# First attention's opening reordered; feed-forward weights quantised inside its loop; layer-norm statistics one sequence per step

## The reference

```python
def _mha(q, k, v, mask):                      # 16 heads of 16 columns
    scores = einsum('bhqd,bhkd->bhqk', qh, kh) / sqrt(16)
    scores = scores + mask[:, None] * -10000.0
    return einsum('bhqk,bhkd->bhqd', softmax(scores), vh)

def lpbq_dequant(w):                          # blocks of 32, 4 bits
    s = maximum(max(abs(wb), axis=-1) / 7, 1e-12)
    return clip(round(wb / s), -8, 7) * s

x = x + _mha(layernorm(x), ctx, ctx, mask)
x = x + ffn(layernorm(x), w_gate, w_up, w_down)   # weights through lpbq_dequant
x = x + xattn(layernorm(x), ctx, ctx, Wq, ...)
x = x + moe(layernorm(x), W1, b1, W2, b2, Wr, br) # 8 experts, top 1
```

## Time and profile before

| what | value |
|---|---|
| median of 3 runs (range) | 1606.71 us (1605.7 to 1612.56) |
| span of the profiled execution | 1606.6 us |
| first attention, first transfer to the start of the feed-forward | 0.8 to 302.8 us |
| start of the first row maximum (step 0) | 40.85 us |
| start of the row maximum of step 4 (first of the loop) | 80.91 us |
| start of the row maximum of step 28 (first behind the loop) | 264.62 us |
| busy over the span: PE, DVE, ACT, POOL | 1336.5, 1215.0, 1030.7, 416.9 us |

### The profile page before, as it was taken

One profiled execution on the slowest core, in us unless ns is written; L12 is line 12 of the kernel. 1 busy time (PEld: TensorE's weight loads), 2 busy tenths in 40 slices (PEclk: granted clock), 3 DMA queues, 4 the chain that ended last, 5 costly groups with the idle time before them and its releaser, 6 DMA issues. The chain is left out here.

```text
span 1606.6 us, 36137 instructions
## 1 busy us (share of the span) xinstructions
PE 1336.5 (83%) x11579; PEld 1171.7 (73%) x11579; DVE 1215.0 (76%) x2159; ACT 1030.7 (64%) x2751; POOL 416.9 (26%) x655
## 2 busy tenths in 40 slices
PE   3688888599973039699999999999999728999996
PEld 2355555488852039688999998999899628999996
DVE  5777777667879997567777777777777777888885
ACT  2578887555578446366676666666667506888885
POOL 2433333100000000402322222222222243555553
PEclk9899999799997569899999999999999859999998
DMA  6411111000042103600111111111100047411110
GB/s 197 152 35 33 39 31 35 15 1 0 0 139 71 39 22 118 208 8 21 34 37 51 34 33 33 33 33 40 39 29 28 21 171 272 153 46 54 50 45 10
DMA packets 61009, 96.76 MB, mean 60 GB/s; under 512 B 9083, under 2 KB 47998, under 8 KB 58113
## 3 DMA queue, kind: packets, MB, share of 16 engines
q1 hardware_dynamic: 55938, 83.15, 15.5%
q0 software_dynamic: 4992, 12.60, 2.5%
HBM read 76.57 MB, written 21.90 MB: 61 GB/s over the span
## 5 line engine op out<-in xcount | busy, mean ns | idle before, releaser
L1695 ACT ACTIVATE c_w_raw<-c_ps_score,c_shift 128x128 f32<-128x128 f32 x512 | 184.6, 397 | 133.0 <-DVE c_shift L1550 130.6
L2081 PE MATMUL d_ps_hT<-d_zT,d_w_tile 128*128 128x128 f32 x1248 | 147.9, 277 | 2.3 <-DVE d_zT L2186 2.3
L2081 PEld LDWEIGHTS d_ps_hT<-d_zT,d_w_tile 128*128 128x128 f32 x1248 | 144.8, 194 | 2.9 <-DVE d_zT L2186 2.9
L840 PE MATMUL b_ps<-b_down_high,b_inner 128*128 128x256 f32 x384 | 71.0, 288 | 89.1 <-DVE b_inner L1122 89.1
L2254 ACT ACTIVATE d_h<-d_ps_hT,d_b1T 128x128 f32<-128x128 f32 x312 | 88.8, 366 | 65.1 <-PE d_ps_hT L2081 65.1
L840 PEld LDWEIGHTS b_ps<-b_down_high,b_inner 128*128 128x128 f32 x384 | 60.6, 194 | 89.5 <-issue 89.5
L2094 PE MATMUL d_ps_y<-d_w_parts,d_hT 128*128 128x256 f32 x936 | 122.9, 288 | 1.8 <-DVE d_res L2217 1.8
L484 DVE TENSOR_REDUCE a_row_max<-a_ps_score 128x8 f32<-128x1024 f32 x64 | 77.9, 1218 | 58.5 <-PE a_ps_score L395 58.5
L1695 ACT ACTIVATION_READ_ACCUMULATOR c_w_raw<-c_ps_score,c_shift 128x1 f32 x512 | 120.9, 236 | 0.0
L2094 PEld LDWEIGHTS d_ps_y<-d_w_parts,d_hT 128*128 128x128 f32 x936 | 115.8, 193 | 2.0 <-DVE d_res L2217 2.0
L1418 PE MATMUL c_ps_proj<-c_ctxT,c_wk 128*128 128x256 f32 x768 | 107.7, 290 | 4.9 <-ACT c_qT L1717 3.3
(11 more groups left out here) (260 smaller groups left out, 3665.7 us busy)
## 6 DMA issues: line engine op xcount, KB each, us to landing
d_w<-w_in SPq DMA_DIRECT2D x16, 1024.0 KB, 7.0
b_x_space<-w_in SPq DMA_DIRECT2D x16, 512.0 KB, 3.5
zx_scratch<-c_zx SPq DMA_DIRECT2D x32, 256.0 KB, 2.4
a_x<-x_in SPq DMA_DIRECT2D x4, 1024.0 KB, 7.5
a_keys<-ctx_blocks_in SPq DMA_DIRECT2D x128, 32.0 KB, 2.1
a_v_raw<-ctx_in SPq DMA_DIRECT2D x4, 1024.0 KB, 8.7
x_scratch<-a_x SPq DMA_DIRECT2D x32, 128.0 KB, 1.7
b_x_space<-x_scratch SPq DMA_DIRECT2D x32, 128.0 KB, 2.4
```

What stands on the lines that cost most here:

```text
L840: last = pe.matmul(ps[:, t, 0:D], inner[:, s, a, f, t * P:(t + 1) * P], down_parts[b][:, f, :], start=(j == 0), stop=(j == NF * len(PARTS) ...
L1695: last = act.activation(prob[:, n, j, :], ps_score[:, n % 2, j, :], ACT.Exp, scale=float(KD) ** -0.5, bias=shift[:, n, j:j + 1], accum_out ...
L2081: last = pe.matmul(ps_hT[:, f, :], w1_tile[:, half, k, n * P:(n + 1) * P], zT[:, s, k, :], start=(k == 0), stop=(k == ND - 1))
```

## The change

- The block for the identity matrix goes; SP loads it second, and PE waits for it ahead of its first transpose.
- SP's opening order becomes: x of sequences 0 and 1, identity, mask, half the keys of the first pair (ACT's queue starts the other half), x of 2 to 7, values, keys of the second pair, the other parts of x and of the mask, and the three weight matrices last. The clearing of the key buffer on POOL is split into two halves.
- The opening quantisation goes. The weights have a buffer of their own, and DVE quantises half a matrix (128 by 768) in each of the 6 passes of the loop: maxima and scale in its first step, reciprocal and product in its second, rounding in its third, product in its fourth. PE's 36 transposes and ACT's copies (now 9 of 512 columns where 36 of 128 were) move into the steps behind the last sequence.
- Statistics for the first eight sequences are taken at the start (two, then six); for the others DVE takes those of sequence b+4 in step b of its loop, and POOL adds two small operations to each step from 4 to 27.

DVE in the opening, before: `w_scale`, `w_inv` are the scales of the weights, `yT` holds the raw weights, `prob` and `probT` serve as scratch.

The diff, cut:

```diff
+        X_PARTS = ((0, 2), (2, 8), (8, 16), (16, 24), (24, 32))
-                load_weights(sp, 0)
-                load_weights(sp, 1)
                 load_x(0)
-                load_weights(sp, 2)
+                sp.dma_start(ident[:], eye).then_inc(ident_loaded, 16)
                 load_mask(0)
-                sp.wait_ge(keys_zero, 1)
-                load_keys(0, 0)
-                load_keys(1, 1)
+                load_first_keys(sp, 0, 0, range(0, HALF, 2))
+                load_x(1)
                 load_v(0)
-                for c in range(1, 4):
+                load_first_keys(sp, 1, 1, range(HALF))
+                for c in range(2, 5):
                     load_x(c)
-                    if c < 3:
-                        load_mask(c)
+                    if c < 4:
+                        load_mask(c - 1)
+                for n, (w, _) in enumerate(weights):
+                    sp.dma_start(w_sb[:, n]..., w...).then_inc(w_loaded, 16)
...
+                def deviation_ahead(b, u):                       # POOL
+                    pool.wait_ge(mv0_done, b + 5)
+                    pool.tensor_tensor(var_next[:, u:u + 1], mv_next[:, u, 1:2], eps[:], ALU.add)
+                    pool.wait_ge(var0_done, b - 1)
+                    pool.tensor_tensor(rstd_next[:, u:u + 1], var_next[:, u:u + 1], power[:, 0:1], ALU.pow)
...
                     if inside(b, 2, NB + 1):
                         residual(b - 2, s)
                         inverse_deviation(b - 2, s)
+                    if inside(b, 4, NB - 5):
+                        deviation_ahead(b, u)
                     if inside(b, 1, NB - 2):
                         values(b + 1, 1 - s)
...
+                def statistics_ahead(b, u):                      # DVE
+                    dve.wait_ge(q_centred, b + 1)
+                    dve.bn_stats(stats_next[:], x_sb[:, b + 4, :]).then_inc(ahead_done, 1)
+                    dve.wait_ge(ahead_done, b - 3)
+                    dve.bn_aggr(mv_next[:, u, :], stats_next[:]).then_inc(mv0_done, 1)
+
+                def quantise(i, u):
+                    half = w_halves[:, bass.ds(i - 1, 1)]
+                    if u == 0:
+                        dve.wait_ge(w_loaded, 16 * MATS)
+                        dve.tensor_reduce(w_scale[:], half, AX_X, ALU.max, ...)
+                        dve.tensor_scalar(w_scale[:], w_scale[:], 1.0 / W_MAX, TINY, ...)
+                    elif u == 1:
+                        dve.reciprocal(w_inv[:], w_scale[:])
+                        dve.tensor_tensor(w_steps[:], half, wide(w_inv), ALU.mult)
+                    elif u == 2:
+                        dve.tensor_scalar(w_rounded[:], w_steps[:], W_MAX, -W_MAX - 1.0, ...)
+                    else:
+                        dve.tensor_tensor(half, w_rounded[:], wide(w_scale), ALU.mult)
+                        dve.wait_ge(w_done, before + 6)
-                quantise_weights(dve)
-                statistics(0)
+                dve.wait_ge(x_loaded[0], 16)
+                statistics(0, 2)
+                dve.wait_ge(x_loaded[1], 16)
+                statistics(2, 8)
                 for b in range(UN):
                     step(b, b % 2)
-                    if b < 3:
-                        statistics(b + 1)
+                for c in range(2, 5):
+                    dve.wait_ge(x_loaded[c], 16)
                 with dve.Fori(1, NB // UN - 1) as i:
                     for u in range(UN):
                         step(UN * i + u, u % 2)
+                        statistics_ahead(UN * i + u, u)
+                        quantise(i, u)
...
                 for b in range(NB - UN, NB + 4):                 # ACT; PE alike
                     step(b, b % UN)
+                    if NB <= b < NB + 3:
+                        copy_weights(*((0, 2), (2, 5), (5, GROUPS))[b - NB])
```

More of the change, by code:

```diff
@@ L57 @@
 MAGIC = 12582912.0
[L60 to L129, removed]
@@ L308, in values @@
                     pool.tensor_copy(v_ones[:, s, :, 0:HD0], src).then_inc(v_ready, 1)
-                pool.memset(keys[:], 0.0).then_inc(keys_zero, 1)
+                for slot in range(2):
+                    pool.memset(keys[:, slot], 0.0).then_inc(keys_zero, 1)
                 pool.memset(power[:], -0.5).then_inc(consts, 1)
@@ new lines, in masks, with queries @@
+                def masks(c):
+                    pool.wait_ge(mask_loaded, 16 * (c + 1))
+                    pool.tensor_copy(mask16[:, 8 * c:8 * (c + 1), :], mask_int[:]).then_inc(mask_ready, 1)
+                def queries(b, s, u):
+                    first = isinstance(b, int) and b < 8
+                    mean, inverse = (mv0[:, b, 0:1], rstd0[:, b:b + 1]) if first else (mv_next[:, u, 0:1], rstd_next[:, u:u + 1])
+                    pool.wait_ge(rstd0_done, min(b // 2 + 1, 2) if first else b - 5)
@@ L461, in step, with turn_weights @@
                             weighted(p, pu, q)
-                weights_copied = turn_weights(pe)
+                def turn_weights(first, end):
+                    for g in range(first, end):
+                        if g == 0:
+                            pe.wait_ge(w_done, OPS * HALVES)
+                        if g >= 4:
+                            pe.wait_ge(w_copied, g - 3)
+                        n, rest = divmod(HB * g, PIECES)
+                        ni = weights[n][0].shape[1] // P
+                        for q in range(HB):
+                            k, o = divmod(rest + q, PIECES // ni)
+                            c = (o * ni + k) * P
+                            last = pe.transpose(w_banks[:, g % 4, q * P:(q + 1) * P], w_sb[:, n, c:c + P], ident[:])
+                        last.then_inc(w_turned, 1)
                 pe.wait_ge(consts, 5)
+                pe.wait_ge(ident_loaded, 16)
                 turn_qy(0, 0)
-                weights_copied()
                 pe.wait_ge(mask_ready, 1)
@@ L536, in step, with statistics @@
                         deviation(b - 2, s)
-                def statistics(c):
-                    dve.wait_ge(x_loaded[c], 16)
-                    for b in range(8 * c, 8 * (c + 1)):
+                def statistics(first, end):
+                    for b in range(first, end):
                         dve.bn_stats(stats0[:, b, :], x_sb[:, b, :]).then_inc(stats0_done, 1)
-                    dve.wait_ge(stats0_done, 8 * (c + 1))
-                    for b in range(8 * c, 8 * (c + 1)):
+                    dve.wait_ge(stats0_done, end)
+                    for b in range(first, end):
@@ L611, in step, with copy_weights @@
                         copy_out(b - 1)
-                copy_weights(act)
+                def copy_weights(first, end):
+                    for g in range(first, end):
+                        n, rest = divmod(HB * g, PIECES)
+                        act.wait_ge(w_turned, g + 1)
+                        act.activation(weights[n][1][:].rearrange("p k n -> p (k n)")[:, rest * P:(rest + HB) * P],
+                                       w_banks[:, g % 4, :], ACT.Copy).then_inc(w_copied, 1)
+                load_first_keys(act, 0, 0, range(1, HALF, 2))
                 copy_qy(0, 0)
```

120 lines of the change are left out of this document (78 added, 42 removed).

## The result

| | before | changed kernel |
|---|---|---|
| median (range) of 4 runs | 1606.7 us (1605.7 to 1612.56) | 1597.12 us (1595.75 to 1601.47) |
| span of the profiled execution | 1606.6 | 1599.7 |
| first row maximum, step 0 | 40.85 | 13.27 |
| row maximum of step 4 | 80.91 | 50.69 |
| row maximum of step 28 | 264.62 | 255.51 |

The ratio is 0.9937, 95% interval 0.9918 to 0.9955: faster by 9.6 us where 20.4 were forecast. The profiled execution is the longest of the four (1601.47 us): its trace shows a gain of 6.9 us by the spans, and its loop is probably longer than that of the median run.

What follows compares the result with a forecast made beforehand. The prediction took DVE to be busiest in the opening and a ring across engines, not one engine, to bound the loop. Terms -30.4 + 4 + 5 + 1 = -20.4 gave 1586 us; range for 8 in 10: 1580 to 1597.

Steps and rivals of the forecast that it cites:

- The opening and steps 0 to 3: First row maximum near 12.8 instead of 40.85 us; maximum of step 4 at 50.5 instead of 80.91: 30.4 us earlier.
- the keys' wait: Ahead of step 4, PE's wait of 6.16 us for the third pair's keys stays, since their order is unchanged.
- B: Transfers bound the opening: at 184 GB/s step 4 starts only 5 us earlier, kernel at 1620 us; chance 0.03.
- D: Opening longer: first maximum at 18 us, or weights delaying the keys; 5 us less gain, 1591 us; chance 0.12.
- the six statistics: In the opening, DVE's other six statistics need x at 9 to 10 us, take 2.6 us and just fit.
- The loop, DVE: Statistics and quantising exceed DVE's slack by 0.22, 0.27, 0 and 0.12 us in a pass's four steps: 4 us in all.
- The loop, DVE against POOL: L488 waits for POOL's shifted query operation: 0.25, 0.3, 0.1 and 0.2 us in four steps, 5 us; ends 0 and 15.
- the sum of the loop: DVE's 4 us and the collisions' 5 us added to the loop; a stretch of 193 us where it was 183.7.
- the prediction's own sign of being wrong: Wrong if the loop grows by over 15 us or less than 4, or step 4 starts later than 55 us.
- the ring: Loop's bound, 7.64 us a step: first row maximum, L488, ACT's exponentials and copies, PE's mask and scores, and back.
- rival A: In the loop the lock costs 12 us in place of 5, register instructions another 5: 1598 us; chance 0.25.
- The end of the block: ACT's nine copies of 512 columns, 5.4 us, end the block 1 us later; ends 0 and 2.5.

Runs made afterwards that it cites:

- run 6: Changed kernel with POOL's two deviation operations one step later, behind the queries, and six idle PE transposes per loop step: 1585.16 us, ratio 0.9861.
- run 11: Changed kernel with idle PE transposes, POOL's two operations behind the queries, and third-pair keys ahead of the last values: 1576.28 us, ratio 0.9808.
- run 12: Run 11 with DVE's wait for its closing product moved to the start of the next half matrix: 1574.35 us, ratio 0.9789.
- run 3: Changed kernel without statistics ahead; sequences from 8 on use those of sequences 0 to 3, quantising stays: 1580.53 us, ratio 0.9829.
- run 2: Changed kernel with six idle transposes of the identity on PE in each of the 24 loop steps: 1588.86 us, ratio 0.9877.
- run 9: Kernel before the change, with one more DVE maximum, result unread, at the end of each loop step: 1623.22 us, ratio 1.0102.
- run 10: Run 9 with six idle transposes of the identity on PE in each loop step: 1613.89 us, ratio 1.0039.
- run 1: Changed kernel without the quantising inside the loop; weights are transposed unquantised: 1590.06 us, ratio 0.9892.
- run 4: Changed kernel with the third pair's keys issued ahead of the last three parts of the values: 1586.41 us, ratio 0.9871.
- run 5: Changed kernel with POOL's two deviation operations one step later, behind the queries: 1592.18 us, ratio 0.9907.
- run 7: Changed kernel with statistics of sequences 8 and up by eight behind steps 1, 2 and 3, none in the loop: 1588.87 us, ratio 0.9888.
- run 8: Run 7 with third-pair keys ahead of the last values and DVE's closing wait moved to the next pass: 1589.39 us, ratio 0.9894.

## Why half of the forecast gain was missing

**The opening and steps 0 to 3: right.** 30.2 us measured, 30.4 forecast, with the intermediate marks within 0.5 us, and the keys' wait kept. The weights didn't hold the queue up, so rivals B and D didn't happen; the six statistics started at 10.75 us, where the walk had their part of x at 9 to 10, and still fitted. B was nearer than the prediction says: the walk's own 13.4 MB by 48.3 us need 277 GB/s, where B is said to decide from about 230, and steps 0 to 3 ran at 290 with the DMA engines busy 0.89 of the time.

**The loop, DVE: the terms of three steps right to 0.16 us, the fourth mis-sized.** Forecast 4 us, measured 191.07 - 183.71 = 7.4 with clock and collisions taken out (run 6). Of this 3.0 are the closing wait with the loop's branch (runs 11 and 12): the fourth step took 8.25 us where the walk gave 7.76. The walk had 0.13 us for it behind the product; it keeps DVE idle for 0.50 us in front of the row maximum. Without it the term is 187.53 - 183.71 = 3.8, with a small collision of the first step in it.

**The loop, DVE against POOL: right in kind, 2.6 to 3.0 us for 5.** I had spread the collision over four steps; it falls on the first alone, with 0.56 us. Since POOL's own operations are stretched by DVE's products, the instants of the query operations couldn't be read by adding 0.77 us to their old places. Nor are POOL's two added operations needed for a collision: run 3 doesn't have them, and its negation was late in two steps of four. The Trainium skill, "SBUF — State Buffer", section "SBUF: two separate sides", says that the port pair is locked for the whole instruction, by a VectorE operation with two SBUF inputs too, against a GpSimd operation that reads SBUF. Its second half, which the trace of before didn't show, agrees with the rows of L559 and L553 above: 0.81 us for 0.19 and 1.25 for 0.55.

**The step that failed is the sum of the loop, which left the clock out.** Forecast +9 us, measured +21.1; the prediction's own sign of being wrong, a loop longer by over 15 us, came true. It walked the ring and took PE's part as constant, without a reason. PE's part isn't constant: when the ring gets longer, PE waits longer in each step, and its clock falls to 1.2 GHz in some of them, which adds 1.1 to 1.6 us to such a step and makes PE the last one. That is the missing term. In the profiled execution it is 10.8 us (run 2) of the 12.8 by which the start of the feed-forward missed the forecast; by the medians it is 8.3 us, or 9.6 by their ratios (0.9937 and 0.9877), of 11. The other deviations, +3.4 us for DVE and -2 for the collisions, partly cancel. That rival A's figure of 1598 lies close to the result is luck, since its cause isn't the one found: the collisions cost 3 us, not 12, and register instructions between dependent operations are within the 3.8.

Its price for one step could have been read: the earlier trace rows has a clock of 0.86 for steps 0 to 3, and the prediction itself used masks of 1.91 and scores of 2.09 us behind waits. How many steps would fall couldn't be read from the kernel before, but the question what 9 us more of waiting do to the clock wasn't asked, and no rival has it. The Trainium skill ("TensorE: Matmul & The Clock Gate", section "Part 1: The HAM clock gate (the "warmup" mystery)") says that the clock follows how busy the array has been recently; that agrees with runs 2, 9 and 10, whose loops had a clock of 0.99, 0.96 and 0.99. In the slow steps of runs 1 to 9 no single wait is over 0.9 us.

**The end of the block: 0 for 1.** The nine copies fitted into ACT's idle time. The 1.5 us behind the loop lie in steps 28 to 31, the first of which runs at the lower clock (8.82 us, and 7.39 in run 2): they are the clock's too.

**What stays open.** Which of the steps fall to the lower clock differs from pass to pass, and in the four runs of one kernel the times spread by up to 12.5 us (run 8). Only one execution of each kernel was profiled, so how many slow steps the median run has isn't shown. Nor is it shown why one step falls and the next of the same kind doesn't. The first step of the loop is the regular case: in the ten profiled kernels in which PE waits 4.4 to 6.5 us for the keys right ahead of it, its clock is 0.79 to 0.94; in the four without that wait (runs 4, 8, 11 and 12) it is 1.00.

## What to carry to other kernels

Where PE waits in a ring with other engines, price a longer ring twice: once for the length itself, and once for steps in which its clock may fall, with masks and scores (or whatever PE has on the path) at nearly twice their time. A few useless matrix operations in PE's wait are a cheap test for it, and here a repair worth 8 to 11 us. After an opening has shrunk, look for the next wait behind it: 6 us for keys queued behind values were still there, and reordering one queue took them away.

## What the runs showed of the hardware

- TensorE's clock fell with no wait of PE above 0.9 us in the step. In the kernel before, PE waited 0.56 and 0.70 us in a steady step of 7.64 us, and the clock held. With waits of 0.77 and 0.70 us in steps of 7.84 (run 9) it fell in four more of 24 steps, and with six transposes in the second of these waits (run 10) it held.
- A step at the lower clock (granted 0.76 to 0.82) took 1.1 to 1.6 us longer than its like at 1.00: 9.67 for 8.53, 9.05 for 7.86 and 9.5 for 7.88 us.
- Adding 144 transposes to PE, about 0.87 us for the six of a step, made the loop 10.8 us shorter.
- A two-input product on DVE (128 by 768, 0.96 us) stretched a POOL operation on one column from 0.19 to 0.81 us, and another from 0.55 to 1.25 us. A rounding with one input (0.56 us) stretched the latter kind to 0.92 us.
- A wait for the engine's own last operation in front of the loop's branch left DVE idle for 0.50 us.
- Eight key transfers took 7.98 us to issue behind three transfers of values, and 5.02 us ahead of them.
